# One turn for the row maxima of two heads, context rows six to a partition, and a new order of steps

## The reference

```python
def reference(x, ctx_1024, ...):
    def _L0_xattn_ref(query, context, ...):
        q = layer_norm(query, gq, betq)
        c = layer_norm(context, gkv, betkv)
        Q, K, V = heads(q @ Wq + bq), heads(c @ Wk + bk), heads(c @ Wv + bv)
        attn = jax.nn.softmax(jnp.einsum('bhqd,bhkd->bhqk', Q, K) * SCALE, axis=-1)
        return merge(jnp.einsum('bhqk,bhkd->bhqd', attn, V)) @ Wo + bo
    def _L0_ffn_ref(x, W1, b1, W2, b2):
        h = jax.nn.relu(jnp.einsum('bsd,fd->bsf', x, _quantize(W1)) + b1)
        return jnp.einsum('bsf,df->bsd', h, _quantize(W2)) + b2
    x = x + jnp.tanh(g_xattn[0]) * _L0_xattn_ref(_layernorm(x), ctx_1024, ...)
    x = x + jnp.tanh(g_ffn[0]) * _L0_ffn_ref(_layernorm(x), ...)
    return x
```

## Time and profile before

| | us |
|---|---|
| median of 3 runs | 974.21 (970.43 to 975.07) |
| the profiled execution, its own time | 970.62 |
| its span in the trace | 968.7 |
| PE busy | 903.6 (93%) |
| DVE busy | 735.1 (76%) |
| ACT busy | 644.0 (66%) |
| POOL busy | 303.6 (31%) |

### The profile page before, as it was taken

One profiled execution on the slowest core, in us unless ns is written; L12 is line 12 of the kernel. 1 busy time (PEld: TensorE's weight loads), 2 busy tenths in 40 slices (PEclk: granted clock), 3 DMA queues, 4 the chain that ended last, 5 costly groups with the idle time before them and its releaser, 6 DMA issues.

```text
span 968.7 us, 22558 instructions
## 1 busy us (share of the span) xinstructions
PE 903.6 (93%) x8996; PEld 693.5 (72%) x8996; DVE 735.1 (76%) x1376; ACT 644.0 (66%) x1330; POOL 303.6 (31%) x519
## 2 busy tenths in 40 slices
PE   2897997889999999999999999999999999889768
PEld 0554665756888688867888688867888688668747
DVE  2667899888688887788688886788677767888521
ACT  1867678656787487657777587757877575678421
POOL 3140375354321343032421344043323223043023
PEclk9999999799999999999999999999999999999979
DMA  9489737550065003340146004440143006110000
GB/s 268 147 245 218 191 99 197 152 124 1 3 143 150 26 2 91 95 134 1 28 117 174 2 2 100 103 117 1 39 106 90 2 2 143 58 33 2 24 19 20
DMA packets 57104, 84.02 MB, mean 87 GB/s; under 512 B 6520, under 2 KB 33592, under 8 KB 57000
## 3 DMA queue, kind: packets, MB, share of 16 engines
q1 hardware_dynamic: 56568, 82.55, 32.5%
q10 hardware_dynamic: 432, 0.02, 0.0%
HBM read 42.20 MB, written 3.67 MB: 47 GB/s over the span
## 4 chain that ended last, share of the span: by engine, by line
PE 80%; DVE 8%; DMA 4%; SPq 3%; ACT 3%; issue 1%; POOL 0%; DVEq 0%; ACTq 0%; POOLq 0%
PE ps_fill L477 52%; PE ps_pv L524 8%; PE ps_score L492 8%; PE ps_exp L508 7%; PE ps_fill L534 4%; DVE row_max L785 2%; SPq L398 2%; DMA h_parts<-w2t 2%; PE ps_fill L583 2%; DVE p_parts L793 2%; DMA ctx_raw<-ctx_in 1%; DMA k_stack<-k_stage_lo 1%; SPq L407 1%; DVE ctx_t_lo L870 1%; DVE bn L825 1%
## 5 line engine op out<-in xcount | busy, mean ns | idle before, releaser
L793 DVE TENSOR_TENSOR p_parts<-ps_exp,p_parts 125x448 f16<-125x448 f32 x384 | 231.7, 618 | 61.8 <-ACT ps_exp L664 59.9
L785 DVE TENSOR_REDUCE row_max<-ps_score 128x1 f32<-128x750 f32 x256 | 239.0, 934 | 46.6 <-PE ps_score L492 45.8
L663 ACT ACTIVATE p_parts<-ps_exp 125x448 f16<-125x448 f32 x384 | 208.9, 544 | 95.2 <-PE ps_exp L508 81.1
L664 ACT ACTIVATE ps_exp<-ps_exp 125x448 f32<-125x448 f32 x384 | 211.0, 549 | 0.0
L492 PE MATMUL ps_score<-k_stack,q_stack 96*128 96x375 f16 x512 | 126.4, 328 | 12.7 <-DVE row_max L785 12.3
L508 PE MATMUL ps_exp<-q_stack,k_stack 99*125 99x224 f16 x768 | 128.1, 266 | 10.2 <-DVE p_parts L793 7.2
L524 PE MATMUL ps_pv<-v_now,p_parts 125*128 125x66 f16 x3072 | 116.1, 194 | 2.4 <-DVE p_parts L793 1.9
L524 PEld LDWEIGHTS ps_pv<-v_now,p_parts 125*128 125x128 f16 x3072 | 110.9, 98 | 8.4 <-DVE p_parts L793 2.1
L477 PE MATMUL ps_fill<-w_ternary,h_parts 128*128 128x256 fp8e4 x1024 | 116.6, 273 | 0.0
L508 PEld LDWEIGHTS ps_exp<-q_stack,k_stack 99*125 99x125 f16 x768 | 87.9, 137 | 34.6 <-DVE p_parts L793 10.1
L477 PEld LDWEIGHTS ps_fill<-w_ternary,h_parts 128*128 128x128 f16 x1024 | 99.7, 98 | 13.2 <-DVE ctx_t_lo L870 1.1
(11 more groups left out here) (139 smaller groups left out, 1549.0 us busy)
## 6 DMA issues: line engine op xcount, KB each, us to landing
k_stack<-k_stage_hi SPq DMA_DIRECT2D x64, 187.5 KB, 2.7
v_now<-v_stage SPq DMA_DIRECT2D x32, 346.5 KB
ctx_raw<-ctx_in SPq DMA_DIRECT2D x8, 1344.0 KB
h_parts<-w1t SPq DMA_DIRECT2D x16, 512.0 KB, 4.5
h_parts<-w2t SPq DMA_DIRECT2D x16, 512.0 KB, 5.0
k_stack<-k_stage_lo SPq DMA_DIRECT2D x32, 187.5 KB, 2.8
x_for_q<-x SPq DMA_DIRECT2D x16, 256.0 KB, 3.7
x_residual<-x SPq DMA_DIRECT2D x16, 256.0 KB, 2.9
```

The lines of the kernel that those rows point to most:

```text
L663: nc.scalar.activation(ph[0:KR, unit, :], ps_exp[0:KR, u, 0:2 * NQ], ACT.Exp, scale=EXP_SCALE)
L664: nc.scalar.activation(ps_exp[0:KR, u, 0:2 * NQ], ps_exp[0:KR, u, 0:2 * NQ], ACT.Exp, scale=EXP_SCALE).then_inc(exp_done, 1)
L785: nc.vector.tensor_reduce(mx[:, i // 2, i % 2:i % 2 + 1], ps_score[:, :, 0:KH], AX.XY, ALU.max) \
L793: nc.vector.tensor_tensor(pl[0:KR, unit, :], ps_exp[0:KR, u, 0:2 * NQ], ph[0:KR, unit, :], ALU.subtract).then_inc(p_split, 1)
```

## The change

1. **mr.** `row_max_parts` is laid out by query half first, so that one matmul turns the parts of two heads: its stationary side has 4 columns (high and low of two heads) where it had 2. A step `mr` has 2 matmuls (128 and 96 columns) where it had 4. ACT copies 4 rows to both heads, and each head's rows of `k_stack` hold -M_SCALE for its own two and 0 for the other's. The stacks have 100 rows where they had 99.
2. **The constant.** SHIFT is added by POOL in the instruction that scales the maxima. The constant row goes, and with it two memsets of POOL at the start; DVE builds `minus_m` with two instructions.
3. **Context rows.** Partition p of `ctx_raw` holds rows 6p to 6p+5, one piece of 12 KB, where it held rows p, p+125, ..., six pieces of 2 KB.
4. **Order.** All three tables are new.

```diff
-STACK_ROWS = MAX_END + 1
+STACK_ROWS = SPLIT_ROWS + 4
...
-        minus_m = sb("minus_m", [48, H * NK // 48], F16)
+        minus_m = sb("minus_m", [32, NK], F16)
+        pick = sb("pick", [32, 1], F32)
...
-        mhl = sb("row_max_parts", [P, H, 2, 2], F16)
+        mhl = sb("row_max_parts", [P, 2, H, 2], F16)
...
-                rows = ctx_in[n].rearrange("(i p) d -> p i d", p=KR)
+                rows = ctx_in[n].rearrange("(p i) d -> p i d", i=KT)
...
-                    for row in range(SPLIT_ROWS, STACK_ROWS):
-                        sp.dma_start(k_flat[row:row + 1, :], minus_m[:, :]).then_inc(rows_set, 16)
+                    sp.wait_ge(minus_ready, 1)
+                    for row in range(4):
+                        sp.dma_start(k_flat[SPLIT_ROWS + row:SPLIT_ROWS + row + 1, :],
+                                     minus_m[1 - row // 2:1 - row // 2 + H, :]).then_inc(rows_set, 16)
...
-                    for h in (2 * i, 2 * i + 1):
-                        for t in range(2):
-                            frm, to = q_cols(t)
-                            last = pe.matmul(
-                                ps_fill[SPLIT_ROWS:MAX_END, bank, (h % 2) * NQ + to.start:(h % 2) * NQ + to.stop],
-                                mhl[:, h, t, :], ident16[:, frm], start=True, stop=True,
-                                tile_position=(0, SPLIT_ROWS))
+                    for t in range(2):
+                        frm, to = q_cols(t)
+                        last = pe.matmul(ps_fill[SPLIT_ROWS:STACK_ROWS, bank, to], mhl[:, t, 2 * i:2 * i + 2, :],
+                                         ident16[:, frm], start=True, stop=True, tile_position=(0, SPLIT_ROWS))
...
-                    nc.scalar.activation(q_stack[SPLIT_ROWS:MAX_END, 2 * i:2 * i + 2, :],
-                                         ps_fill[SPLIT_ROWS:MAX_END, bank, 0:2 * NQ]
-                                         .rearrange("p (h n) -> p h n", h=2), ACT.Copy).then_inc(shift_rows, 1)
+                    nc.scalar.activation(q_stack[SPLIT_ROWS:STACK_ROWS, 2 * i:2 * i + 2, :],
+                                         ps_fill[SPLIT_ROWS:STACK_ROWS, bank, 0:NQ].unsqueeze(1)
+                                         .to_broadcast([4, 2, NQ]), ACT.Copy).then_inc(shift_rows, 1)
...
-                nc.gpsimd.tensor_scalar(mx[:, h2, :], mx[:, h2, :], 1.0 / M_SCALE, None, ALU.mult) \
+                nc.gpsimd.tensor_scalar(mx[:, h2, :], mx[:, h2, :], 1.0 / M_SCALE, -SHIFT, ALU.mult, ALU.add) \
...
-            nc.gpsimd.memset(minus_m[:, :], -M_SCALE).then_inc(consts, 1)
-            nc.gpsimd.memset(q_stack[SPLIT_ROWS:STACK_ROWS, :, :], -SHIFT).then_inc(consts, 1)
```

## The result

| | before | changed |
|---|---|---|
| median, us | 970.7 (969.7 to 975.07, 5 runs) | 992.56 (991.16 to 994.67, 5 runs) |
| ratio to before | | 1.0189, 95% interval 1.0157 to 1.0222 |
| span of the profiled execution | 968.7 | 989.4 |

The two medians alone stand at 1.0225; both that and the ratio on record say that the changed kernel is slower by about 2%. A few executions of the kernels that follow were disturbed and far slower than the others (1063.67 us in e1, 1329.71 in e3, 5111.48 in e7), which the ratios leave out and the medians count (966.70, 991.85 and 972.45 without them), and e3's trace, taken in such an execution, isn't read.

The account below looks back on a forecast made before the run. PE was taken as the bound in rounds 2 to 6, waits at both ends; -6.1 -2.0 -2.0 -1.7 +3.2 = -8.6 from the 974.21 median gave 965.6 us, own range 959 to 970, 8 in 10 range 955 to 982.

Parts of the forecast that it names:

- The mr step: PE, 64 steps: two matmuls where there were four take each from 0.29 to 0.19 us, -6.1 us in all.
- Rival E: The mr step gives nothing, its time being change of engine set-up and not columns: 972 us, chance 0.10.
- The context load: Contiguous context rows load faster: -2.0 us at the start, and up to 1.5 us earlier in a round.
- The opening: At batch 2's context load: sending kq.3@0 earlier and a faster load shorten DVE's and PE's waits, -2.0 us.
- the ending: At pv.15@7: f2.3@6 now ahead of it covers its 1.71 us wait for DVE, -1.7 us.
- The rounds: Rounds 2 to 5: later context, store and xb make PE wait 0.8 us at mr.2 each, +3.2 us, bounds 0 to 10.8.
- rival D: Slower: mr.2 waits 2.7 us in each of four rounds, with lower clock behind: 981 us, chance 0.13.
- the signs that I had named for it: PE idle over 2 us a round, or the clock in the middle below 1.00, would point to rival D.
- the last one on my list: Sign of being wrong: an engine other than POOL holds a PE step in the middle, DVE being nearest.
- Rival C: Context layout doesn't matter: start gains 0, opening 1, a hole of 1.3 us a round; 971 or 976 us, chance 0.17.
- Rival B: Fast context and no hole at mr.2, with full gains at start, opening and ending: 958 us, chance 0.18.

Follow-up runs that it names:

- e1: The changed kernel with the three order tables and context rows of before, leaving the mr step and SHIFT: 967.76 us, ratio 0.9955.
- e3: The changed kernel with the old context rows, six pieces of 2 KB: 994.17 us, ratio 1.0227.
- e7: The changed kernel with SP's order of a round and the places of cx.5 and cx_lo.5 as before: 972.82 us, ratio 0.9995.
- e2: The kernel before with the new context rows and nothing else: 973.77 us, ratio 1.0028.
- e9: e1 with kq.3@0 moved ahead of batch 2's context load and vc.0 to vc.2 in the opening: 968.54 us, ratio 0.9958.
- e8: e1 with f2.3@6 moved between the last expo and pv.15@7: 968.03 us, ratio 0.9955.
- e5: The changed kernel with only SP's order of each round as before (x, vc.2 ahead of kq.3, vc.3 behind the store): 987.28 us, ratio 1.0156.

## Why the prediction was wrong, by its own steps

- **The mr step, -6.1.** Right in mechanism and sign, about a quarter too large: 4.9 us by the rounds of e1 and before (0.61 a round, not 0.77), 4.8 by the medians, 4.4 by the ratio. The step is 0.19 in the chain as said; where the other 0.16 a round goes isn't known. That the spans differ by just 6.1 is luck. Rival E falls, as the interval of e1's ratio stays below 1.
- **The context load, -2.0 at the start and up to 1.5 a round.** Wrong; it is 0. The step that failed is "what differs is that context pieces of one partition lie 125 rows apart in memory": they no longer do, and the rate is 171 GB/s from 10 to 14 us of the changed kernel, against 168. The rule cited from the Trainium skill, "DMA: Bandwidth & Descriptors", Specifications, which asks for no more than 512 B, gave the right sum for this term: e2 agrees that longer pieces bring nothing, with 173, though neither 168 nor 173 is the 401 GB/s of the weights. What does hold the rate at 168 while the DMA engines are full was not found.
- **The opening, -2.0, and the ending, -1.7.** Both 0 for the moves named (e9, e8). The waits named did go, and came back one step away. The new opening as a whole is no gain either: it reaches `mr.1@2` at 310.43, and the old one with the same `mr` step at 305.87 to 307.94 (e1, e8, e9). A wait of 1 to 2 us beside a DVE or a DMA queue that has no room isn't a gain that stands there to be taken.
- **The rounds, +3.2, with 0 to 10.8 as bounds.** This is the term that made the forecast wrong. Its mechanism was right, its size was not: five rounds lost 22 us, though the mr step gave 0.6 back in each. Checked in the round shown, against `mr.1` at 423.02, the context load was said to go out 1.9 us ahead of it, and did 2.1 ahead (420.90). From xb's issue to `mr.2` I had 7.6 us, and it was 7.56 (434.00, 441.56). Between the two lies the step that failed: "xb goes out between 423.5 and 426.4", 5 to 8 us behind `mr.1`; it was 11.0 here, and 8.2, 9.7 and 10.2 in the other rounds. I took the store's 9.0 us as the upper bound and only took off from it, for V's copies moved ahead. It was 12.2 here and 9.5 to 11.5 in the others. V and x, moved to right ahead of the context load, hadn't drained when it started, and e5 prices them at 3.5 us here and 2.1 on average. I had listed x's new place in the change and given it no price.
- So `mr.2` itself stands 10.3 us in four rounds: three times the 3.2 forecast, but still inside the bound of 10.8. The other 5.8 us of idle time and some 6 us of lower clock are outside it, and for these two the term had no entry.
- The second miss of the same term: I let only `mr.2` wait. `op_add.0` and `stat.0` wait 2.92 and 2.49 us on DVE in the round shown, and `q_hi.0` 1.38.
- The third: the sum has full clock behind every hole in the rounds. I had seen half the clock behind the 2.40 us hole and left it to rival D.
- **Rival D** had the right place, side and mechanism, with 981 us and a chance of 0.13. It has `mr.2` wait 2.7 us a round, 10.8 in all, and it was 10.3; it has 8 us for a lower clock behind the holes, and it was some 6, in three rounds of four. It is still 11.6 us short, for two reasons: 5.8 us of idle time at other steps, and the 11.8 us of savings that it takes over from my forecast, of which only the 4 to 5 of the mr step came. Both of the signs that I had named for it came: PE is idle over 2 us in each round, and the clock is below 1.00 in the middle. So did the last one on my list: DVE too holds PE steps there, at the `expo` and at a score.
- **Rival C** was right about its condition (the layout doesn't matter; the first statistics at 14.98), and too low with 971 to 976 by the price of the rounds. **Rival B** falls with the fast context that it needed.

By the parts, against e1, which has the same `mr` step, and by the traces: up to `mr.1@2` 4.6 us later, from there to `mr.1@6` 24.1 more, behind it 1.9 less, together the 26.8 between their spans. The first and the last of these vary by some 2 us from execution to execution; the middle one is the loss.

The version that beats both kernels is e1, the mr step in the old order: 0.9955 (0.9927 to 0.9983).

## What to carry to other kernels

When a load is made later, price what now stands ahead of it on the DMA engines, and let the landing of whatever is queued behind it grow; the time it took in the old place is not an upper bound. A step that sends a load is worth most where it releases a chain (here a single `ctx_raw` and a single `x_residual`), so look for the steps that wait for its landing on every engine, not only for the one on PE. Price a hole in PE's work with the lower clock behind it, if a trace of the kernel shows one. And test a good part of a change alone: a gain of 4 to 5 us in one part was here under a loss of some 25 in another.

## What the runs showed of the hardware

- A load of 1536 KB in 12 KB contiguous pieces and one in 2 KB pieces take the same: 171 to 173 GB/s against 168 in the same stretch of the start, with DMA engines at a share of 0.91 to 1.08. It is first used at 14.49 and 14.98 us against 14.80.
- A hole of 2 to 3 us in PE's work can bring the lower clock, and doesn't always: in the changed kernel the clock is 0.55 to 0.59 for the 4 to 8 us behind idle times of 2.55, 1.91 and 3.08 us, and 1.00 from 548 to 556 around one of 3.18 us. Before, with PE busy for 118.7 to 120 us of each 120, it is 1.00 in all windows from 240 to 840.
- The end of a train of loads is long. Windows of the changed kernel, while SP waits for the store and DVE for the context:

```profile
426.00:430.00 4.00, 4.00 (x30) 2.83 (x29) 2.35 (x6) 2.75 (x6) 0.90 (x1) 1.00 0.91 220
430.00:434.00 4.00, 3.16 (x15) 1.13 (x13) 1.51 (x4) 0.57 (x1) 0.00 (x0) 1.00 0.20 73
```

In the last 4 us the 16 engines are busy for a share of 0.20 only, and both DMAs land in it, the context by 432.89 and the store at 433.98. So it isn't the mean rate that sets a landing here. That it is the engines that finish last is what this suggests; which ones, and why, wasn't looked at.
